# Attention with a pair's two heads on rows 0-63 and 64-127 of TensorE's array

## The reference

```
xn = layernorm(x)
q  = (xn @ wq) as 32 heads of 16;  k = xn @ wk;  v = xn @ wv     # one key and value head for all
s  = softmax(causal(q @ k.T / 4)) @ v;   s = s @ wo
h  = linear8bit(xn, W1, b1)        # 512 -> 2048, int8-like rounding by rows, outlier columns apart
g  = silu(linear8bit(h, W2, b2))   # 2048 -> 512
out = x + s * g
```

## Time and profile before

| | |
|---|---|
| median of three runs | 802.34 us (799.99 to 802.61) |
| the profiled execution, its time | 802.84 us |
| its span | 801.1 us |
| PE busy | 764.9 us, 95% |
| PE weight loads busy | 579.5 us, 72% |
| DVE busy | 638.7 us, 80% |
| ACT busy | 402.7 us, 50% |
| POOL busy | 257.6 us, 32% |
| costliest group | DVE line 914, 384 reductions, 210.9 us |

### The profile page before, as it was taken

The page is one execution under the profiler, slowest core; times in us unless marked ns, Lnnn a source line. Parts: engine busy times, 40 slices in busy tenths (PEclk is TensorE's granted clock), DMA queues, the critical chain, the costliest instruction groups (busy, mean ns, idle before and its releaser), DMA issues. The chain is left out here.

```text
span 801.1 us, 12089 instructions
## 1 busy us (share of the span) xinstructions
PE 764.9 (95%) x4253; PEld 579.5 (72%) x4253; DVE 638.7 (80%) x1094; ACT 402.7 (50%) x683; POOL 257.6 (32%) x335
## 2 busy tenths in 40 slices
PE   4999999999999999999999999999997999999995
PEld 3877665556676666775578888788886788888884
DVE  7988989999999899995537476666658998599957
ACT  3454166767677676777634554544553333122212
POOL 7313135555555555554621110110100000036504
PEclk9999589999999999999999999999999999999998
DMA  7421303333322223334554444222013778536982
GB/s 258 153 106 53 86 11 91 82 80 92 90 81 83 82 81 95 89 113 123 161 192 159 143 158 144 81 78 79 27 47 97 251 220 259 164 106 219 334 287 105
DMA packets 58348, 103.37 MB, mean 129 GB/s; under 512 B 8480, under 2 KB 16688, under 8 KB 56752
## 3 DMA queue, kind: packets, MB, share of 16 engines
q1 hardware_dynamic: 58288, 102.60, 40.3%
HBM read 52.76 MB, written 36.70 MB: 112 GB/s over the span
## 5 line engine op out<-in xcount | busy, mean ns | idle before, releaser
L914 DVE TENSOR_REDUCE rowmax<-ps 128x2 f32<-128x512 f32 (+3 forms) x384 | 210.9, 591 | 20.7 <-PE ps L991 18.8
L835 ACT ACTIVATE probs<-ps 128x512 f32<-128x512 f32 (+1 forms) x352 | 175.2, 557 | 72.4 <-PE ps L1004 70.7
L991 PE MATMUL ps<-km,stack 128*128 128x256 f32 (+3 forms) x512 | 151.0, 350 | 2.0 <-PEq L187 1.9
L1004 PE MATMUL ps<-stack,ks 128*128 128x512 f32 (+1 forms) x352 | 133.1, 388 | 2.6 <-ACT probs L835 2.6
L991 PEld LDWEIGHTS ps<-km,stack 128*128 128x128 f32 (+1 forms) x512 | 96.0, 201 | 42.2 <-DVE rowmax L914 22.5
L817 POOL TENSOR_SCALAR_AFFINE_SELECT probs<-probs 128x512 f32<-128x512 f32 x128 | 81.0, 641 | 79.1 <-ACT probs L835 77.6
L1806 PE MATMUL ps<-big_h 128*128 128x512 f32 x256 | 100.4, 392 | 2.4 <-issue 2.0
L1808 PE MATMUL ps<-big_h,big_l 128*128 128x512 f32 x256 | 100.3, 392 | 0.0
L1807 PE MATMUL ps<-big_l,big_h 128*128 128x512 f32 x256 | 100.2, 391 | 0.0
L1017 PE MATMUL ps<-probs,vones 128*32 128x512 f32 (+3 forms) x1024 | 82.2, 439 | 0.2 <-POOL probs L817 0.2
L1004 PEld LDWEIGHTS ps<-stack,ks 128*128 128x128 f32 x352 | 67.5, 192 | 11.9 <-ACT probs L835 6.3
(11 more groups left out here) (227 smaller groups left out, 1384.3 us busy)
## 6 DMA issues: line engine op xcount, KB each, us to landing
stack<-big_h SPq DMA_DIRECT2D x128, 64.0 KB, 2.0
h_scratch<-hs SPq DMA_DIRECT2D x7, 1024.0 KB, 4.5
hload<-h_scratch SPq DMA_DIRECT2D x14, 512.0 KB, 5.4
xn_scratch<-xa SPq DMA_DIRECT2D x4, 1024.0 KB, 4.4
stack<-big_l SPq DMA_DIRECT2D x64, 64.0 KB, 2.0
xi<-xn_scratch SPq DMA_DIRECT2D x16, 256.0 KB, 2.8
...
```

Of the source, the lines that this page charges most:

```text
L835: nc.scalar.activation(probs[p][:, o:o + nh * w], ps[:, STB[n % NST], 0:nh * w], ACT.Exp).then_inc(s_exp, 1)
L914: nc.vector.tensor_reduce(dst, src, AX_X, ALU.max).then_inc(s_red, 1)
L991: last = nc.tensor.matmul(dst, stack[u % 3][rows, hp, P * qt:P * (qt + 1)], km[rows, u // KT, p0:p0 + npar, keys], start=True, stop=True)
L1004: ins = nc.tensor.matmul(ps[:, STB[n % NST], 0:nh * w].rearrange("p (h q) -> p h q", h=nh), ks[:, u // KT, p, P * kt:P * (kt + 1)], stack[ ...
```

## The change

**Rows of the array.** A pair's two heads (a = 0 and 1) now have stack partitions 0-63 and 64-127, in each half 16 high, 16 low, 16 high and 16 spare. The keys `km` and `ks` are held once a batch, with the same content in both halves, and not once for each head of the pair. Each product takes 64 partitions (48 where it needs no spare rows) and is issued for a = 0 and then for a = 1, each into its own bank.

**Pieces.** `max_pair` replaces `max_piece`: 20 pieces a unit, each filling a bank of 512 columns, issued as ten pairs, with products of 384, 256 and 128 columns. `score_pair` replaces `scores`: again 20 pieces of 512 columns in ten pairs. `CH` is 20, `LAG` 10. A pair waits until the reduction (or the exponential) two pieces back from its first is done. The groups of `pv` are key tiles (0, 1, 3) and (2).

**Transfers.** For one DMA to bring the queries of all four pairs, the features of q are put in another order, by head, dimension and pair: the weight copies of wq read and write with strides (`by_head`, `in_features`), and `wo` is loaded in eight pieces whose rows are permuted to match. A unit's queries take 6 transfers of 128 KB in place of 12 of 64 KB, the maxima 2 in place of 1. There are four stacks. The whole stack is filled with `later_q` before its queries come.

**Tables.** `later_q` and `later_k` have ten steps of 2^12 in place of five of 2^25, and each is copied to the second half. In preparation DVE makes one key product a batch in place of two, and the key and value weights are copied in four pieces in place of two.

The diff, cut to its core:

```diff
-SPARE, RUN, STEP = 100, 5, 2.0 ** 25
+SPARE, RUN, STEP, OWN = 50, 10, 2.0 ** 12, 32.0
...
         def fill_spare(i):
...
+            return nc.gpsimd.tensor_copy(stack[i][:, :, :].rearrange("r h (j k) -> r (h j) k", k=P),
+                                         later_q[:, :].rearrange("r (o k) -> r o k", o=1)
+                                         .broadcast_to([P, NPAIR * QT, P]))
...
-            for hp in range(NPAIR):
-                src = slice(2 * HD * hp, 2 * HD * (hp + 1))
+            for a in range(2):
+                src = slice(HALF_ROWS * a, HALF_ROWS * (a + 1))
                 for n, part in enumerate((big_h, big_l, big_h)):
...
+                    lo = HALF_ROWS * a + HD * n
+                    sp.dma_start(stack[u % NSTK][lo:lo + HD, :, :].bitcast(F32),
+                                 part[src, f, tok].bitcast(F32)).then_inc(s_sq[u % NSTK], 16)
...
+        def in_features(row):
+            return row.rearrange("p (f h x) -> p f h x", f=KT, h=NPAIR)
+        def by_head(row):
+            return row.rearrange("p (f x h) -> p f h x", f=KT, h=NPAIR)
...
+                            wo_rows = wo.rearrange("(k p) n -> p k n", p=P)
+                            for h2, h1, a in itertools.product(range(2), repeat=3):
+                                to, of = 2 * HD * (2 * h1 + a) + HD * h2, 2 * HD * (2 * h2 + h1) + HD * a
+                                sp.dma_start(wo_in[to:to + HD], wo_rows[of:of + HD]).then_inc(s_wload["wo"], 16)
...
                 steps_along(later_q, [STEP ** -s for s in range(RUN)] + [0.0])
...
                 fill_spare(0).then_inc(s_z, 1)
                 pool.wait_ge(s_z, 1)
+                steps_along(later_k, [-OWN * STEP ** t for t in range(RUN + 1)])
...
+                    nc.gpsimd.tensor_tensor(km[:, g, :].rearrange("r (j k) -> r j k", k=P),
+                                            ks[:, g, :].bitcast(F32).rearrange("r (j k) -> r j k", k=P),
+                                            later_k[:, :].rearrange("r (o k) -> r o k", o=1)
+                                            .broadcast_to([P, QT, P]), ALU.add).then_inc(s_ks, 1)
+                    pool.wait_ge(s_ks, g + 1)
+                    nc.gpsimd.tensor_tensor(ks[:, g, :], ks[:, g, :].bitcast(F32),
+                                            cols[:, 2:3].broadcast_to([P, T]), ALU.add).then_inc(s_kz, 1)
...
                 for k in range(KT):
-                    weight_low(wql[:, k, :], wq_in[k], wqh[:, k, :], 3 + k)
+                    weight_low(by_head(wql[:, k, :]), in_features(wq_in[k]), by_head(wqh[:, k, :]), 5 + k)
...
-                        for p in range(2):
-                            step(nc.vector.tensor_scalar(km[:, g, p, :], kvh, cols[:, p:p + 1], None,
-                                                         ALU.mult))
-                            ins = nc.vector.scalar_tensor_tensor(out=km[:, g, p, :], in0=kvl,
...
+                        step(nc.vector.tensor_scalar(ks[:, g, :], kvh, cols[:, 0:1], None, ALU.mult))
+                        ins = nc.vector.scalar_tensor_tensor(out=ks[:, g, :], in0=kvl, scalar=cols[:, 1:2],
+                                                             in1=ks[:, g, :].bitcast(F32),
+                                                             op0=ALU.mult, op1=ALU.add)
...
-        CH = 24
...
-        PIECES = [[(0, True, 0, 2)], [(1, False, 0, 2), (1, True, 0, 2)], [(2, False, 0, 2)],
-                  [(2, True, 0, 2), (3, True, 0, 2)], [(3, False, 0, 1)], [(3, False, 1, 1)]]
-        BANKS = [(0, 0, 1), (0, 1, 1), (0, 2, 1), (0, 3, 1), (1, 0, 1), (1, 1, 1), (1, 2, 1), (1, 3, 1),
-                 (2, 0, 2), (2, 2, 2), (3, 0, 4)]
-        NB = len(BANKS)
-        KT_END = [4, 8, 10, 11]
-        GROUPS = [(0, 1), (2, 3)]
+        CH, NB = 20, 10
...
+        def pieces_of(c):
+            v, m = divmod(c // 2, 5)
+            hp = 2 * v + m // 2
+            if m == 4:
+                return [(2 * v + h, 1, own, 2 * P * h + P * own) for h in range(2) for own in (False, True)]
+            if m % 2:
+                return [(hp, 2, False, 0), (hp, 2, True, 2 * P), (hp, 0, True, 3 * P)]
+            return [(hp, 3, False, 0), (hp, 3, True, 3 * P)]
+        def scores_of(i):
+            return [[(0, 0, 1, 0)], [(0, 1, 1, 0)], [(1, 0, 1, 0), (3, 0, 1, 3 * P)],
+                    [(1, 1, 1, 0), (3, 1, 1, 3 * P)], [(2, 0, 2, 0)]][i]
+        def scores_at(i, a):
+            return ((0, 2 * T, OF_1, OF_1 + 2 * T, OF_2)[i]) + T * a
+        def probs_of(kt, j):
+            h, a = divmod(j, 2)
+            return {0: T * j, 1: OF_1 + T * j, 3: OF_1 + T * j + 3 * P, 2: OF_2 + T * a + 2 * P * h}[kt]
+        MASK_END = {4: (0,), 8: (1, 3), 10: (2,)}
+        MASK_OF = {0: 0, 1: 1, 3: 2, 2: 3}
+        GROUPS = [(0, 1, 3), (2,)]
...
-        LAG = 11
+        LAG = 10
...
-        PV_AT = {11: (0, 0), 16: (0, 1), 22: (1, 0), 27: (1, 1)}
-        NORM_AT = {19: 0, 27: 1, 30: 2, 33: 3}
-        SHARE_AT, HIGH_AT, LOW_AT = 30, 34, 33
-        XLOAD_AT, XMASK_AT, XSCALE_AT, XROUND_AT, XBACK_AT, XSTORE_AT = -1, 15, 21, 25, 26, 30
+        PV_AT = {10: (0, 0), 14: (0, 1), 18: (1, 0), 22: (1, 1)}
+        NORM_AT = {16: 0, 24: 1, 26: 2, 29: 3}
+        SHARE_AT, HIGH_AT, LOW_AT = 25, 29, 28
+        XLOAD_AT, XMASK_AT, XSCALE_AT, XROUND_AT, XBACK_AT, XSTORE_AT = -1, 12, 16, 21, 22, 26
...
+                    if u < NSTK:
+                        sp.wait_ge(s_z, u + 1)
+                    else:
+                        sp.wait_ge(s_st, 2 * NB * (u - NSTK + 1))
                     stack_queries(sp, u)
...
+                    for a in range(2):
+                        lo = HALF_ROWS * a + KEPT
+                        sp.dma_start(stack[u % NSTK][lo:lo + 2, :, :].bitcast(F32),
+                                     mhl[HPF * a:HPF * (a + 1), :].bitcast(F32)).then_inc(s_sm[u % NSTK], 16)
...
+                    if g == LAG + 1:
+                        queries(NSTK - 1)
                     u = unit_at(g, 2 * NB + 1)
-                    if 0 <= u < U - 3:
-                        queries(u + 3)
+                    if 0 <= u < U - NSTK:
+                        queries(u + NSTK)
...
+                        of = NPAIR * (c % 2) + 2 * v
+                        if m == 4:
+                            src, dst = bank.rearrange("p (h k) -> p h k", h=2), mine[:, QT, of:of + 2]
+                        elif m % 2:
+                            src, dst = bank.rearrange("p (s k) -> p s k", k=P), mine[:, 0:QT, of + m // 2]
                         else:
-                            qt, _, p0, npar = PIECES[m][0]
-                            w = P * (qt + 1) if qt < 2 else P * qt
-                            src = bank[:, 0:npar * w].rearrange("p (a k) -> p a k", a=npar)
-                            dst = mine[:, qt, :].rearrange("p (a h) -> p a h", a=2)[:, p0:p0 + npar, hp]
+                            src, dst = bank, mine[:, QT + 2, of + m // 2:of + m // 2 + 1]
                         nc.vector.tensor_reduce(dst, src, AX_X, ALU.max).then_inc(s_red, 1)
...
-                def max_piece(u, c):
-                    hp, m = divmod(c, 6)
+                def max_pair(u, c):
...
                         pe.wait_ge(s_z, u + 1)
-                    if m == 0:
...
-                    if n >= NMAX:
-                        pe.wait_ge(s_red, n - NMAX + 1)
...
-                        rows = slice(0, P if own else 6 * HD)
+                    if c == 0:
+                        pe.wait_ge(s_sq[u % NSTK], 16 * 6 * (u // NSTK + 1))
+                    if n + 1 >= NMAX:
+                        pe.wait_ge(s_red, n + 2 - NMAX)
+                    pieces = pieces_of(c)
+                    for hp, qt, own, at in pieces:
...
-                def scores(u, s):
-                    p, i = divmod(s, NB)
-                    kt, h0, nh = BANKS[i]
-                    w = T - P * kt
+                        for a in range(2):
+                            rows = slice(HALF_ROWS * a, HALF_ROWS * a + (HALF_ROWS if own else KEPT))
+                            dst = ps[:, MAXB[(n + a) % NMAX], at:at + keys.stop - keys.start]
+                            ins = nc.tensor.matmul(dst, stack[u % NSTK][rows, hp, P * qt:P * (qt + 1)],
+                                                   km[rows, u // KT, keys], start=True, stop=True)
+                            if (hp, qt, own, at) == pieces[-1]:
+                                ins.then_inc(s_max, 1)
...
+                def score_pair(u, s):
+                    p, i = divmod(s // 2, NB // 2)
                     n = 2 * NB * u + s
                     if s == 0:
...
+                        pe.wait_ge(s_sm[u % NSTK], 32 * (u // NSTK + 1))
+                    if n + 1 >= NST:
+                        pe.wait_ge(s_exp, n + 2 - NST)
+                    parts = scores_of(i)
+                    for kt, h, nh, at in parts:
+                        w = T - P * kt
+                        for a in range(2):
```

(7 more changed lines are left out.)

181 lines of the change are left out of this document (68 added, 113 removed).

## The result

The changed kernel took **814.58 us** (median of 4 runs, 812.62 to 815.83) against 802.05 for the kernel before on the same chip; the ratio is 1.0159, with a 95% interval of 1.0131 to 1.0186. The forecast was 793: wrong in sign, and 21.6 us off. The profiled execution has a span of 813.7 us.

What follows compares the result with a forecast made beforehand. TensorE was taken to bound the kernel, with VectorE close behind and the bound after the change. Terms -12.8 + 2.3 + 0.3 + 1.0 = -9.2 us from 802.84 gave 793; likeliest case 785 to 801, whole range 784 to 829.

Steps and rivals of the forecast that it cites:

- The clock falls: Rival, steady stretch: TensorE, no longer full, is clocked down for a tenth of it; some 10 us more, 803; chance 0.04.
- the row at 0.60 clock: Profile row for 80 to 110 us, mean granted clock 0.60; the prediction took TensorE as mostly idle, doing only maxima.
- Unit 17.4 for 18.28: Attention units: VectorE's 16.0 plus waits of 0.3 and 1.1 make 17.4 us instead of 18.28; 12.8 us gained over 14.5 units.
- TensorE 14.8: TensorE's work per attention unit falls from 18.3 to 14.8 us, with maxima at 3.4 and scores at 2.6.
- The first 30 steps, +2.3: Start of attention, maxima only at low clock: pairs come 0.2 us late each; 2.3 us lost (0.7 gained to 5 lost).
- Before attention, +0.3, up to 2.4: Preparation: more small weight copies and strided query-weight copies lose 0.3 us, up to 2.4 if strided writes took twice as long.
- The last steps, +1.0: Attention's end, without maxima: two of three score banks bound together lose 1 us (1 gained to 2 lost).
- Short pairs at 0.22: Rival, maxima and scores: a pair of 128-column products costs 0.22 us instead of 0.11; 826 us; chance 0.24.
- no overlap: Rival, maxima and scores: the two halves of a pair do not run side by side; 845 us; chance 0.06.
- All given back: Rival: waits reach 1.9 us a unit (unit 17.9), first and last steps lose 5 us; 802 us; chance 0.11.
- Transfers: nothing: Query and maxima transfers: fewer issues and a ring of four change nothing; the second maxima transfer's 0.6 us stays hidden.

Runs made afterwards that it cites:

- e12: e11 without the groups of three unread products in the units that have no projection; 807.15 us, ratio 1.0071 to the kernel before.
- e11: e10 with two of the four low parts of the queries' weights made later, behind the first transposed inputs; 795.82 us, ratio 0.9946 to the kernel before.
- e7: Changed kernel plus groups of three unread full-array products where later units have projections, only from step 47 on; 805.09 us, ratio 1.0050 to the kernel before.
- e10: e5 with the fourth stack filled later, after the copies of the first unit's maxima; 798.88 us, ratio 0.9984 to the kernel before.
- e2: Changed kernel with the queries' weights copied in their own order, without strided writes (heads in wrong places); 812.90 us, ratio 1.0141 to the kernel before.
- e1: Changed kernel plus groups of three unread full products in the first six units, where later units have projections; 812.95 us, ratio 1.0143 to the kernel before.
- e8: e7 with the queries' weights permuted by strided reads instead of strided writes; 804.72 us, ratio 1.0047 to the kernel before.
- e14: e11 with one unread product instead of three in each of its places in the units; 798.66 us, ratio 0.9954 to the kernel before.
- e6: Changed kernel with both heads' products read from rows 0-63, so none on different array halves; 1014.88 us, ratio 1.2682 to the kernel before.
- e9: Changed kernel with the fourth stack filled after the copies of the first unit's maxima; 814.21 us, ratio 1.0177 to the kernel before.
- e5: Changed kernel plus unread products on TensorE: eight after the last queries' product, two behind each of the first 15 pairs, later groups of three; 808.02 us, ratio 1.0088.

## Why the prediction was wrong, by its own steps

- **The clock falls** was a rival with a chance of 0.04, "some 10 us on top". It is what happened: e12 against e11 gives 11.3 us in the 262 us stretch, e7 against the changed kernel 8.7. The failed step is the sentence against it, "it would still be occupied for 14.8 of 17.4 us". That is the value of a unit with a projection; the first six have none, about 2.8 us of products fewer, which by the forecast's own prices leaves 12.0. The other failed reading is of the row at 0.60 clock. The prediction called TensorE "mostly idle" there, but the same row has it busy for 28.47 of 30 us: a high busy share beside a low clock stood in the rows already, and was read as a property of the first steps and not as a warning. The prediction's last paragraph does name a clock under 1.00 behind 110 us as the sign of a failure: it was seen at 0.76 to 0.84.
- **Unit 17.4 for 18.28:** 17.4 is right where the clock is full (17.41). Partly that is luck: of its terms, the waits were 0.8 a unit for the 1.4 taken, 4.7 us in 12 waits over six units,
```profile
DVE rowmax L945 <- PE ps L1018: 4.7, 12, 0.4
```
  and VectorE's own part is then 16.6 for 16.0. The 18.28 is right for units with a projection alone: the kernel before spent 17.53 on each of the first three that its timeline gives, from 125.1 us on, and 18.24 to 18.30 on the later ones, so there was less to gain early than "14.5 x (18.28 - 17.4)" has it. With full clock throughout (e10, e11) the stretch took 251.1: -11.3 for the forecast's -12.8.
- **TensorE 14.8** was mis-sized. In the same six units it stood idle ahead of the maxima for 3.5 us, 0.6 a unit, so it was occupied for 16.8. By the distances in one unit (250.7 to 268.2 us) maxima take 3.9 for the 3.4 of the sum, scores 3.9 for 2.6, projection 3.6 for 2.8, transposes 0.6 for 0.4, and the value groups 4.9 as forecast. The short pairs were a little dearer than taken (six products 0.40 for 0.34). The rest, some 2 us, is put down to the change between half-array and full-array products. The prediction had 0.7 of it in the sum, taken over from the kernel before, and left about 1 us in a sentence beside it. The slack hides it: no unit at full clock grew by it.
- **The first 30 steps, +2.3:** measured +5.7 in the changed kernel and +1.4 with the clock held up (e10). The kernel before had run its first steps at the same low clock almost without a wait of VectorE; here a pair costs 1.5 to 2.0 us at 1.2 GHz; I had added only 0.2 a pair for it.
- **Before attention, +0.3, up to 2.4:** measured +3.4. Strides took 1.9 times the time on ScalarE and 1.4 times on VectorE (against e2), the upper bound was the better value, and the later start met a low clock (0.43 us from product to product at 17.7 us instead of 0.23).
- **The last steps, +1.0:** +3.9 up to the first FFN product. No run takes it apart, but the traces do in part. TensorE stands idle for 7.5 us there, where the kernel before has 4.5. Its waits for exponentials are 2.0 us for 0.2: two of three score banks bound together cost more than the 1 taken for it. One wait for a transfer is 2.09 us where the kernel before had 0.98; it is 0.4 to 0.8 in e1, e8, e12 and e14, and with it the stage is 47.9 to 48.2. In e10 and e11 it is short too, but 3 to 4 us of low clock stand in its place (49.0).
```profile
396.66 0.66 PE L1111 MATMUL ps<-ident,tail_rows 128*128 128x128 f32 x4 [2.09 <-DMA tail_rows<-xe_scratch]
404.25 0.50 PE L1036 MATMUL ps<-stack,ks 64*128 64x512 f32 x2 [0.96 <-ACT probs L868]
```
- **Short pairs at 0.22** are refuted by the changed kernel's rows (eight products of 128 columns, four pairs, take 0.50), **no overlap** by e6. **All given back** had a mean unit of 17.9 where the stretch gives 18.1, but by waits of the pairs, and it was the clock. **Transfers: nothing** held in the changed kernel (e9) and failed as soon as the first steps were fast (e5, e10): 8 to 9 us lie between these two.
- **"From 785 to 801"** is not what the terms' bounds give. Added up as they stand (33 gained to 10 lost, 0.7 gained to 5 lost, 0 to 2.4 lost, 1 gained to 2 lost) they reach from 768 to 822, which holds the 814.58.

Sum, changed against before: +3.4 +5.7 -0.2 +3.9 -0.2 = +12.6, the difference of the spans. With the clock held up through the first steps and the units (e10): +3.6 +1.4 -11.3 +3.2 -1.3 = -4.4; and the median of e10 is only 0.2% below the kernel before. So the clock explains why the sign was wrong, and not the whole of the 21.6 us.
